# Head scores of a four-layer gated cross-attention kernel: two-part 32-bit operands on 64 rows a head in place of three-part bf16 on 100 rows

## What is computed

```python
x = x + jnp.tanh(g_xattn[0]) * _L0_xattn_ref(_layernorm(x, axis=-1), ctx_1024, ...)   # and so in layers 1, 2
    q = x @ Wq.T + bq
    k = context @ Wk.T + bk          # layer 1: rotary turn of q and k
    v = context @ Wv.T + bv
    q = q.reshape(B, T, H, d).transpose(0, 2, 1, 3)          # H = 16, d = 16, T = 512
    scores = jnp.einsum('bhtd,bhcd->bhtc', q, k) / jnp.sqrt(jnp.asarray(d, x.dtype))
    attn = jax.nn.softmax(scores, axis=-1)                   # over 1601 keys
    out = jnp.einsum('bhtc,bhcd->bhtd', attn, v)
    return out.transpose(0, 2, 1, 3).reshape(B, T, D) @ Wo.T + bo
```

## Time and profile before

| | |
|---|---|
| median of 3 runs | 4376.03 us (4375.51 to 4383.13) |
| the profiled execution | 4381.18 us |
| its span, first to last instruction | 4380.0 us |
| mean granted TensorE clock | 0.916 |
| layer 0: first score tile of the second pass to the last | 139.4 to 907.0 us |
| layer 1, the same | 1165.7 to 2009.7 us |
| layer 2, the same | 2407.9 to 3190.2 us |

### The profile page before, as it was taken

How to read it: one execution, slowest core, us unless ns; L and a number is a source line. 1 busy time by engine, 2 the same in 40 slices (tenths; PEclk the granted TensorE clock), 3 DMA queues, 4 the chain that set the end, 5 groups by cost and what they waited for, 6 DMA issues and landing times. The chain is left out here.

```text
span 4380.0 us, 54568 instructions
## 1 busy us (share of the span) xinstructions
PE 3603.8 (82%) x19622; PEld 1953.4 (45%) x19622; DVE 2138.6 (49%) x3325; ACT 2104.0 (48%) x4606; POOL 737.1 (17%) x764
## 2 busy tenths in 40 slices
PE   3999999965698989896865989898959698893993
PEld 2334343343242424233862434343339366593993
DVE  4766666646656565673016666666530211242332
ACT  1566666631365555563322666666723222251662
POOL 1111121013060505101120212030010200003103
PEclk8999999987899999997987999999969799996997
DMA  6242415013515151502546151515034100122555
GB/s 131 42 61 45 68 46 69 1 56 85 72 54 61 60 67 58 68 1 97 181 148 98 38 68 39 68 46 60 1 132 166 57 15 15 45 69 95 182 182 107
DMA packets 215237, 323.62 MB, mean 74 GB/s; under 512 B 40034, under 2 KB 156195, under 8 KB 214587
## 3 DMA queue, kind: packets, MB, share of 16 engines
q1 hardware_dynamic: 185754, 215.00, 24.8%
q0 software_dynamic: 29216, 105.14, 7.8%
HBM read 253.42 MB, written 65.17 MB: 73 GB/s over the span
## 5 line engine op out<-in xcount | busy, mean ns | idle before, releaser
L631 DVE TENSOR_REDUCE mxp<-m 128x1 f32<-128x802 f32 x1536 | 1454.4, 988 | 730.2 <-PE m L731 728.1
L839 ACT ACTIVATE e_t<-s 128x512 f32<-128x512 f32 (+1 forms) x2496 | 1361.6, 599 | 734.1 <-PE s L750 732.6
L731 PE MATMUL m<-kaug,qaug 97*128 97x401 bf16 x3072 | 801.6, 343 | 221.4 <-DMA kaug<-maskrow 132.4
L750 PE MATMUL s<-qaug,kaug 100*128 100x512 bf16 (+1 forms) x2496 | 873.7, 387 | 20.6 <-ACT e_t L839 11.8
L761 PE MATMUL pv<-e_t,v 128*32 128x512 f32 (+1 forms) x4992 | 673.4, 612 | 0.2
L750 PEld LDWEIGHTS s<-qaug,kaug 100*128 100x128 bf16 (+1 forms) x2496 | 237.4, 101 | 700.0 <-ACT e_t L839 457.2
L731 PEld LDWEIGHTS m<-kaug,qaug 97*128 97x128 bf16 x3072 | 281.9, 100 | 594.1 <-DVE mxp L631 164.1
L1642 PE MATMUL y<-w,hT 128*128 (+1 forms) x1504 | 346.8, 385 | 11.7 <-DVE hT L1499 11.7
L1633 PE MATMUL h<-xtT,w 128*128 128x128 f32 x2496 | 297.5, 278 | 10.9 <-DMA w<-in_L_w 7.3
L1642 PEld LDWEIGHTS y<-w,hT 128*128 128x128 f32 x1504 | 283.2, 193 | 48.9 <-issue 6.4
L1633 PEld LDWEIGHTS h<-xtT,w 128*128 128x128 f32 x2496 | 290.9, 195 | 12.2 <-issue 12.0
(11 more groups left out here) (274 smaller groups left out, 3480.4 us busy)
## 6 DMA issues: line engine op xcount, KB each, us to landing
w<-in_L_w POOLq DMA_DIRECT2D x78, 1024.0 KB, 5.4
kaug<-kparts SPq DMA_DIRECT2D x252, 200.1 KB
kparts<-ks SPq DMA_DIRECT2D x66, 384.0 KB, 3.1
w<-in_L_w SPq DMA_DIRECT2D x24, 1024.0 KB, 13.0
ctxb<-in_ctxT SPq DMA_DIRECT2D x33, 512.0 KB, 4.6
qaug<-qparts SPq DMA_DIRECT2D x216, 64.0 KB
xt<-xs SPq DMA_DIRECT2D x78, 128.0 KB, 2.3
ys<-y SPq DMA_DIRECT2D x78, 128.0 KB, 1.7
```

The lines of the kernel that those rows point to most:

```text
L631: dve.tensor_reduce(a.mxp[:, u.g % 2, half, n:n + 1], a.m_slot[u.m % 2][:].rearrange("p (a n) -> p a n", a=2)[:, :, 0:PIECE + 1], AX.XY, A ...
L731: m = pe.matmul(slot[:, 512 * k:512 * k + PIECE + 1], a.qaug[0:R_MAX, u.g, j, P * qc:P * qc + P], a.kaug[0:R_MAX, u.g, j, k0:k0 + PIECE + ...
L750: pe.matmul(slot[0:KW[u.k], :], a.kaug[0:R_ALL, u.g, u.j, P * u.k:P * u.k + KW[u.k]], a.qaug[0:R_ALL, u.g, u.j, :], start=True, stop=True) ...
L839: act.activation(a.e_t[0:KW[u.k], e % 2, u.j, :], a.s_slot[u.s % 3][0:KW[u.k], :], ACT.Exp).then_inc(s_free.sem, 1)
```

## The change

The parts are now f32 values of type float32r (`F32R`), which TensorE multiplies in a single pass instead of the passes of plain f32. q and k are split into two parts (high, low) instead of three, three products of parts instead of six, so a head needs 16 x 3 rows, the mask row and two rows for the maximum: 51 rows (49 in the maxima). Two heads of a group stand in one tile: heads 0 and 2 of a group on rows 0 to 50, heads 1 and 3 on rows 64 to 114. The heads of a step go in the order 0, 2, 1, 3, and `maxima` takes each unit from a head on the half other than that of the score tile before it. The pieces of the maxima are 402 wide. `head_split` has one or two operations instead of three or four; ACT writes the high part itself only in batch 0 of layers 0 and 2. At a layer's start the keys of batch 0 are projected ahead of the norm (unit `ln`), in layer 1 the first four of eight tiles; the first fetch brings the keys of two groups, and q comes after it. `x + bob` leaves DVE's `out` and is done once a layer for all tokens on POOL (`xbias`). The constant rows come from a DRAM tensor; the mask row is one DMA for each half instead of one for each head; a turn is 4 DMAs instead of 3; the zero tile of layer 0's feed-forward part moves there.

```diff
-RUNS = ((0, 0, 3), (3, 1, 2), (5, 2, 1))
-R_MASK = 16 * 6
+RUNS = ((0, 0), (1, 0), (0, 1))
+R_MASK = 16 * 3
 R_MAX = R_MASK + 1
-R_ALL = R_MAX + 3
+R_ALL = R_MAX + 2
+HALF = P // 2
+ORDER = (0, 2, 1, 3)
-PIECE = 400
+PIECE = 402
+PIECES = (0, 400, 800, 1199)
...
     def maxima(self, g, b, begin=0, end=2 * HG * QC + 2):
+        left = self.left.setdefault((b, g), [[k for k in range(2 * HG * QC) if k // (2 * QC) % 2 == half] for half in range(2)])
         for i in range(begin, min(end, 2 * HG * QC)):
-            self.add("max", b=b, g=g, k=i)
+            half = 1 - self.half
+            self.add("max", b=b, g=g, k=(left[half] or left[1 - half]).pop(0))
...
-            for j in range(HG):
+            for at, j in enumerate(ORDER):
                 self.add("s2", b=b, g=g, k=k, j=j)
+                self.half = j % 2
...
-        for _ in self.project(0, ("dve",), "q"):
-            pass
-        for n, _ in enumerate(self.project(0, ("pool", "dve", "dve"), "k")):
-            if n == 3:
-                self.add("fetch", b=0, g=0, what="q", k=NG, by="kd3")
-        self.add("fetch", b=0, g=0, what="k", k=1, by="kd0")
+        self.add("begin", b=0, what="kq")
+        keys = [(c, n_c) for c in range(DC) for n_c in range(len(CHUNKS))]
+        if self.rope:
+            keys = [(c, n_c) for n_c in range(len(CHUNKS)) for c in range(DC)]
+        for n, (c, n_c) in enumerate(keys):
+            self.split("k", 0, c, n_c, ("pool",) if not self.rope or n < 4 else ("dve",))
+            if not self.rope and n == 3:
+                self.add("fetch", b=0, g=0, what="k", k=2, by="kd0")
+            if self.rope and n == 3:
+                self.add("ln")
+        if self.rope:
+            self.add("fetch", b=0, g=0, what="k", k=2, by="kd0")
+        else:
+            self.add("ln")
+        for c in range(DC):
+            self.split("q", 0, c, 0, ("dve",))
+        self.add("fetch", b=0, g=0, what="q", k=NG, by="kd3")
+        self.add("fetch", b=0, g=2, what="k", k=2, by="kd2")
...
-        a.kaug = sb("kaug", [P, NG, HG, S2], BF16)
-        a.qaug = sb("qaug", [P, NG, HG, T], BF16)
+        a.kaug = sb("kaug", [P, NP, S2], F32R)
+        a.qaug = sb("qaug", [P, NP, T], F32R)
...
-    split3(kn, eng, own, kn.cst["ones"][:, 0:1].to_broadcast([P, n]), o, src, [ks[:, k, 0:n] for k in range(3)],
-           a.rope is None and not live).then_inc(done.sem, 1)
+    high, low = ks[:, 0, 0:n], ks[:, 1, 0:n]
+    if not split_direct(a, u):
+        kn.settle(eng, own, eng.tensor_tensor(high, src, kn.cst["ones"][:, 0:1].to_broadcast([P, n]), ALU.mult))
+    eng.tensor_tensor(low, src, high.bitcast(F32), ALU.subtract).then_inc(done.sem, 1)
...
+def split_direct(a, u):
+    return u.b == 0 and a.rope is None and not (a.mask is not None and u.kind == "q")
...
             dve.scalar_tensor_tensor(xt, a.m_slot[u.m % 2][:, 0:D], a.gate, xt, ALU.mult, ALU.add).then_inc(m_free.sem, 1)
-            dve.wait_ge(m_free.sem, m_free.at(u.m + 1))
-            i = dve.tensor_tensor(xt, xt, a.bob[:], ALU.add)
...
+            r0, pair = HALF * (j % 2), 2 * u.g + j // 2
             for k in range(2):
-                k0 = PIECE * (2 * half + k)
-                m = pe.matmul(slot[:, 512 * k:512 * k + PIECE + 1], a.qaug[0:R_MAX, u.g, j, P * qc:P * qc + P],
-                              a.kaug[0:R_MAX, u.g, j, k0:k0 + PIECE + 1], start=True, stop=True)
+                k0 = PIECES[2 * half + k]
+                m = pe.matmul(slot[:, 512 * k:512 * k + PIECE], a.qaug[r0:r0 + R_MAX, pair, P * qc:P * qc + P],
+                              a.kaug[r0:r0 + R_MAX, pair, k0:k0 + PIECE], start=True, stop=True)
...
-            pe.matmul(slot[0:KW[u.k], :], a.kaug[0:R_ALL, u.g, u.j, P * u.k:P * u.k + KW[u.k]],
-                      a.qaug[0:R_ALL, u.g, u.j, :], start=True, stop=True).then_inc(s_full.sem, 1)
+            r0, pair = HALF * (u.j % 2), 2 * u.g + u.j // 2
+            pe.matmul(slot[0:KW[u.k], :], a.kaug[r0:r0 + R_ALL, pair, P * u.k:P * u.k + KW[u.k]],
+                      a.qaug[r0:r0 + R_ALL, pair, :], start=True, stop=True).then_inc(s_full.sem, 1)
```

More of the change, by code:

```diff
@@ L295, in lay_out @@
         self.add("bias")
+        for b in range(B):
+            self.add("xbias", b=b)
         for g in range(NG):
@@ L454, in head_sp @@
         context(0, n_c, n_c)
-    spread = lambda t: t.rearrange("p (a n) -> p a n", a=1).to_broadcast([t.shape[0], H, t.shape[1]])
-    sp.wait_ge(filled.sem, filled.at(1))
-    for t, n in ((a.kaug, S2), (a.qaug, T)):
-        sp.dma_start(t[R_MASK:R_ALL, :, :, :].rearrange("p g j n -> p (g j) n"),
-                     spread(a.fill[0:R_ALL - R_MASK, 0:n])).then_inc(rows.sem, DMA)
-        n_of("rows")
-    sp.wait_ge(rows.sem, rows.at(2))
-    if a.mask is None:
-        sp.dma_start(a.kaug[R_MASK:R_MASK + 1, :, :, :].rearrange("p g j n -> p (g j) n"),
-                     spread(a.fill[0:1, S2:2 * S2])).then_inc(rows.sem, DMA)
-        n_of("rows")
+    for half in range(2):
+        r0 = HALF * half
+        for to, r, k, row_of, n in ((a.kaug, R_MAX, 2, w["one_row"], S2), (a.qaug, R_MASK, 1, w["one_row"], T),
+                                    (a.kaug, R_MASK, 1, w["zero_row"], S2)):
+            if to is not a.kaug or r != R_MASK or a.mask is None:
+                sp.dma_start(to[r0 + r:r0 + r + k, :, :].bitcast(F32),
+                             row_of[:, 0:n].rearrange("a (b n) -> a b n", b=1).to_broadcast([k, NP, n])).then_inc(rows.sem, DMA)
+                n_of("rows")
     loads = []
@@ L534, in head_sp @@
             sp.wait_ge(m_free.sem, m_free.at(u.m + 1))
-            for k in range(3):
-                sp.dma_start(a.qaug[R_MAX + k:R_MAX + k + 1, u.g, :, :].rearrange("a j (c q) -> a (j c) q", q=P),
-                             a.tm[16 * k:16 * k + 16, :]).then_inc(td.sem, DMA)
-def split3(kn, eng, own, one, rest, src, parts, have):
-    if not have:
-        kn.settle(eng, own, eng.tensor_tensor(parts[0], src, one, ALU.mult))
-    kn.settle(eng, own, eng.tensor_tensor(rest, src, parts[0], ALU.subtract))
-    kn.settle(eng, own, eng.tensor_tensor(parts[1], rest, one, ALU.mult))
-    return eng.tensor_tensor(parts[2], rest, parts[1], ALU.subtract)
+            for k in range(2):
+                for half in range(2):
+                    r0, t0 = HALF * half + R_MAX + k, HG * QC * k + HG * QC // 2 * half
+                    sp.dma_start(a.qaug[r0:r0 + 1, 2 * u.g:2 * u.g + 2, :].rearrange("a j (c q) -> a (j c) q", q=P).bitcast(F32),
+                                 a.tm[t0:t0 + HG * QC // 2, :].bitcast(F32)).then_inc(td.sem, DMA)
 def head_split(kn, a, u, eng, name):
```

158 lines of the change are left out of this document (87 added, 71 removed).

## The result

The changed kernel takes **4706 us** (median; 4688 to 4714) where the kernel before took 4380 in the same comparison: ratio 1.074, 95% interval 1.070 to 1.078. It is 7% slower; the forecast was 4164, and 4706 lies far above the range. The profiled execution has a span of 4701.7 us.

What follows compares the result with a forecast made beforehand. PE was taken as the bound in the head layers, with DVE and ACT waiting. Groups -217, mode changes +30 and starts -25 sum to -212 us, from 4376 to 4164 us; range 4030 to 4350.

Steps and rivals of the forecast that it cites:

- Number and cost of columns: Score passes: same 2496 tiles and 3072 maxima; a single-pass 32-bit column costs as bf16, 0.22 us per 512 columns.
- Rival 3: Score passes slower: a 32-bit column costs two times 0.22 per 512, giving 4570 us or 1085 more; chance 0.07.
- Side by side: Score matmuls on two row halves overlap: at most 11.3 us saved per full group, 4.5 taken (40.5 to 36.0).
- Rival 2: Score matmuls on the two halves go one after another: 4340 to 4400 us, say 4365; chance 0.15.
- 51 rows instead of 100 save nothing in themselves: Score matmuls: price goes by columns, so fewer rows alone change nothing; clock expected at 1.00.
- Weight loads: Score steps: 9 loads cost PE up to 0.38 us a step or nothing; allowed for in the group's middle value.
- Rival 1: Halves meet with gaps: mode changes paid in full (30 more), 32-bit loads take back 70; 4264 us, chance 0.22.
- Passing between halves and the full array: Full-array work between half-row matmuls: about 430 changes at 0.14 us, 60 us, half hidden, so 30 us against.
- Starts: Layer starts up to first maximum, keys before norm: 25 us gained (3 in layers 0 and 2, 19 in layer 1).
- The sum: Whole kernel: -217 (groups, three layers) + 30 (mode changes) - 25 (starts) = -212 us, giving 4164 us.

Runs made afterwards that it cites:

- run 4: Changed kernel with every 32-bit score matmul reading both heads' rows on the full array, one after the other: 4535 us, ratio 1.035.
- run 3: Changed kernel with each half filled to 64 rows by zeros, which the score matmuls read: 4546 us, ratio 1.038.
- run 1: Kernel before with score matmuls on 49 rows (maxima) and 51 (tiles) instead of 97 and 100, still bf16: 5260 us, ratio 1.198.
- run 2: Kernel before with score matmuls on 65 rows instead of 97 and 100: 4764 us, ratio 1.089.
- run 9: Changed kernel with old start order and halves zero-filled to 64 rows: 4479 us, ratio 1.025; then also score operands read as bf16: 4382 us, ratio 1.002.
- run 5: Changed kernel with score operands read as bf16 (upper two bytes), same rows and halves: 4431 us, ratio 1.010.
- Run 8: Changed kernel with the old order at a layer's start (norm and queries first, one group of keys fetched ahead): 4619 us, ratio 1.057.

## Why the prediction was wrong

- **Number and cost of columns: right.** Three tiles in a row take 0.96 us in 32 bits on the full array (run 4) and 0.82 in bf16, where a second pass over each column would add 0.66 (an estimate, 3 x 0.22); a tile costs 0.23 in the stream, 0.22 in bf16, and has one record (L776 x2496), where a plain 32-bit product has two of 0.43. Rival 3 is out.
- **Side by side: right in mechanism.** Starts 0.01 us apart, one tile of three hidden. Rival 2 is out. In a full group it saves 2.8 to 3.3 us of the 11.3 that could shrink, not 4.5: the size was off by a third.
- **"51 rows instead of 100 save nothing in themselves": the step that failed.** They save nothing, they cost: I put nothing down for what fewer rows do to the clock and priced every group at 1.00, and the clock is not at 1.00 (0.85, 0.84 and 0.87 in the groups of the three layers, before 0.98, 0.97 and 0.98). What I took for it was the 1.00 of the last group of before. That group ran on 100 rows. The error was to carry the clock of one set of operands over to another. The window at 177.5 shows PE busy 60.13 of 60.20 us at 0.50. Size: 194 of the +216 in groups (run 3), and some 60 of the +67 in the maxima phases (run 4 has 51.1, 46.7 and 46.1 us there, at 0.77 to 0.83; run 1, with fewer rows and nothing else, has 68.9, 65.3 and 65.4). A wait is not all that the clock follows: it falls to 0.50 in the waits for keys of 7.0 and 7.1 us (before and run 2), but run 1, with PE busy 73.70 of 73.70 us at 0.50, and run 3, where rows of zeros lift the groups from 0.85, 0.84 and 0.87 to 0.97, 0.95 and 0.95, show that the rows of the operands count as well.
- **Weight loads: right in kind, missing in the sum.** Rival 1 had up to 0.38 a step, 4.9 a group; the sum had no term for them, only a middle that should allow for them. Run 4 has 2.9 us a full group at clock 1.00, run 9 2.4 to 2.5 in halves. That is all that side by side saves, which is why 40.2 equals 40.5. One load takes 0.21 us in the 32-bit form (the change) and 0.10 in bf16 (run 5, on the same rows); how much of the 2.4 to 2.9 is the loads' was not tried apart.
- **Passing between halves and the full array (rival 1's change of mode): +30 put down, about that found.** The first projection group takes 19.6 us more than a full one in run 3 (59.7 and 40.1) and 17.5 in run 4 (60.9 and 43.4), which has no half-row scores: 2.1 us for its 16 projections, sum and norm, 0.12 each, near the 0.14 that I took. In bf16 the same comparison, 19.5 us in run 9 (57.2 and 37.7) and 18.4 before (58.9 and 40.5), gives 1.1 us, 0.06 each. Over my 430 changes that is 26 to 52 us, an estimate.
- **Starts: forecast -25, found +35** up to the first maximum. I had seen that the queries come last and twice the keys are fetched. What I missed is in PE's order: the transposes of the norm stand behind key tiles that wait for split buffers, 23.7 us in layer 2. Run 8 splits it: order +63, the rest of the change -28.
- **The sum**: -217 became +216, +30 is within it, -25 became +35, and +67 stood nowhere in my list, since I had not costed the maxima phase, which has the same matmuls on few rows. With most of the clock given back (run 3) the groups stand at +22 and not at -217: the 32-bit form takes what side by side saves, and that is the second error, in size, beside the clock.

## What to carry to other kernels

Before you cut the contraction rows of a matmul that streams for long, ask what the granted clock does: read the clock of a window in which PE is full with the new operands, not with the old ones. If the rows are few, fill them with zeros and measure: here it cost no PE time (40.2 and 40.1 us a full group at clock 1.00) and gave most of the groups' clock back (0.95 to 0.97, from 0.84 to 0.87), for 13 to 18 us a layer of DMAs ahead of the first maximum; it did not help the maxima phase (0.50 to 0.53 with it and without). And price a new operand type by its load beside its stream: side by side saved 3.3 us a full group, and the 32-bit form cost 2.9 (2.4 to 2.5 on halves).

## What was not expected of the hardware

- The granted clock depends on the number of rows and on what went before. Full groups behind a wait for keys in layer 0 ran at 1.00 on 97 and 100 rows, at 0.63 on 65, and at 0.50 on 49 and 51, with PE busy 39.77 of 40.50, 59.70 of 59.90 and 73.70 of 73.70 us. Without a wait ahead of it, one on 65 rows ran at 1.00, PE busy 39.70 of 40.50 us (run 2). Rows of zeros count as rows: the groups of layer 0 are at 0.97 with them (run 3) and at 0.85 without.
- Side by side the same rows do better: in bf16 on 49 and 51 rows the mean clock is 0.867 with the halves in turns (run 5) and 0.745 with all on the first rows (run 1).
- At 51 rows side by side the clock is not steady: full groups of the change last 40 us at 1.00 in one place and 50 to 58 at 0.76 to 0.59 in others, with the same instructions, and the kernel's runs spread over 27 us, those of the kernel before over 11.
- Zero-filled halves of 64 rows had 0.95 to 0.97 in the groups but 0.50 to 0.53 in the maxima phase at the start of a layer, where no tiles stand beside the maxima. In layer 0 the same phase had 0.52 on 49 rows, 0.81 on 65 and 0.77 on 113. Why 64 is enough in one and not in the other, and whether it is the row or the half array that decides there, was not settled.
